# Three steps of shared experts among the first attention's rounds, and 26 instead of 18 sums of gathered rows left to the second attention

## Chip, cores and metric

One core of one Trainium2 chip runs the whole program, in float32, as one launch. The metric is the device time of one launch in microseconds; the time given for a kernel is the median of several runs.

## What is computed

Two decoder layers run on x of 4 x 1024 rows of 256 columns (NT = 4096 rows), with a context of 4 x 77 rows. A layer is an attention over the rows, a cross attention to the context and a mixture of experts, each with a residual and a layer norm behind it:

```python
x = _layernorm(x + _L0_attn_ref(x, ...))            # retention, 8 heads
x = _layernorm(x + _L0_xattn_ref(x, ctx, ctx, ...)) # 16 heads, 77 context rows
x = _layernorm(x + _L0_ffn_ref(x, ...))             # 64 experts, top 8, and 2 shared experts
x = _layernorm(x + _L1_attn_ref(x, ...))            # linear attention with a memory
x = _layernorm(x + _L1_xattn_ref(x, ctx, ctx, ...))
x = _layernorm(x + _L1_ffn_ref(x, ...))             # 8 gated experts, top 2

# in _L0_ffn_ref
h = jax.nn.silu(xf @ W1 + B1) @ W2 + B2             # one routed expert, 256 -> 64 -> 256
routed = sum over experts of cw[:, None] * h        # cw: weight of the expert, 0 unless in the row's top 8
shared = jnp.sum(jax.vmap(shared_mlp)(sw1, sb1, sw2, sb2), axis=0)   # 2 experts, 256 -> 512 -> 256, all rows
return routed + shared
```

## The kernel before

The rows are cut into 8 steps (STEPS) of 512 rows (128 of each of the 4 batches). The program has four phases, one behind the other, with some work let across the borders.

**First attention** (`attention_phase` with layer 0). The list SEQUENCE0 (L208) names the stages of a round, each with how many rounds ahead its step is; `steady` (L165) writes the rounds out, so that retention of step n, cross attention of step n-1, the router of step n-2 and the scatter of step n-3 share a round. All engines go through that one order. The stages that the change touches or stands beside: "cwt" and "b2" (expert weights turned, times the routed experts' second bias, plus the shared bias, into the tile `x2s`, which is the start value "base" of the feed phase's output and goes to memory by rows), "qk", "mx" (scores, L1186), "kt", "ret", "sc" (L1199 and L1202, scores of the cross attention), "mix" (L1069 and L1074), "pv" (L1212), L1057 (retention's part "ret"), and "put", in which GpSimd scatters each row eightfold into `lists`, the rows sorted by expert (L597, from round 3 on). SyncE's queue fills `lists` with zeros ahead of that (20 stores of 2 MB), loads the rows of later steps and stores x2, its transpose and the routes. A job's PSUM bank comes from one of two rings (`bank_jobs`: "wide" for "ret", "mx" and "sc", otherwise "narrow"). The prefetch of the routed experts' first weights (`prefetch(sp, 0)`, 4 MB) is issued at the phase's start. At its end `with_units` puts the first 8 units of the shared experts.

**A unit** (class `SharedExperts`) is one 128-column slice of the shared experts' 1024 hidden columns for one step: `inward` (L110, two matmuls of 512 columns, counted as four instructions in the profile), `activate` (L118, Silu on ScalarE) and `outward` (L127, four matmuls of 256 columns, counted as eight). Eight units (UNITS) make a step, 64 units (TOTAL) all; after the eighth, VectorE adds the result to base (L1697, "base"), and base goes back to memory ("send").

**Feed phase** (`feed_phase`, order by `feed_order` L1268). First 20 units (FIRST_UNITS), then 80 quads. A quad is four pages of 128 sorted rows: transposed on TensorE (L1716), times the first weights (L1728), Silu, times the second weights (L1739), stored to `results`. From quad 24 on (`begun`), a unit stands behind four of each five quads, a "weigh" (the second weights scaled, L1684 to L1690) behind each, and a sum behind six of seven. A sum adds one of the eight experts' results to a step's 512 rows: GpSimd gathers 4 x 128 rows of `results` (L1441, four DMA_INDIRECT for a sum, after a `rest` of L158), VectorE multiplies them by the weights and adds them (L1456, four instructions); after eight sums a step is done and its layer norm follows, so there are 64 sums. The first sum of step s waits until 24 + 8s quads are stored. LATE = STEPS*K0 - 18 = 46 sums are in this phase:

```python
units(FIRST_UNITS)
for j in range(QUADS0):
    order.append(("quad", j))
    ...
        weights(1)
        units(0 if (j - begun) % 5 == 0 else 1)
    if j >= begun + 2 and (j - begun) % 7:
        sums(1)
```

**Second attention** (`attention_phase` with layer 1, order SEQUENCE1). `with_late` puts the sums that the feed phase left, 18 here, behind named stages of its first rounds (the list `behind`); GpSimd's gathers for them run three sums ahead (AHEAD).

**Gated experts** (`gated_phase`): 8 experts of layer 1, matmuls of L2067 and L2079.

## Time and profile before

| | us |
|---|---|
| median of three runs | 1869.29 |
| lowest and highest | 1869.01, 1887.16 |
| span of the profiled execution | 1981.9 |
| profiled execution against the median | 112.6 longer |

The profiled execution is one launch with the hardware profiler on, and its span is the time from its first to its last instruction; the profile's times are of that launch. By the starts of its lines the first attention lies at 41 to about 600 us, the first units' end at 685, quads 0 to 23 at 685 to 776, quads 24 to 79 at 776 to 1107, the end of the feed phase to 1171, the second attention up to about 1500 and the gated experts behind it. PE is TensorE, DVE VectorE, ACT ScalarE, POOL GpSimd, SP SyncE. PEclk is the TensorE clock granted, 1.00 being 2.4 GHz and 0.5 being 1.2 GHz; "issue" as the releaser of a wait means that the engine waited for nothing that the profile shows.

### The profile page before, as it was taken

The page shows a single profiled execution, that of the slowest core. Times are in us where ns is not written, and L with a number is a line of the kernel's source. Part 1 is how long each engine was busy: PE and PEld are TensorE (multiplying, and loading weights), DVE is VectorE, ACT ScalarE, POOL GpSimd, SP SyncE. Part 2 cuts the span into 40 slices and gives each one's busy share as a digit, 9 for nine tenths or more (in the row PEclk, how much of TensorE's full clock was granted, in tenths as well). Part 3 has the DMA queues.
Part 4 walks back from the last instruction along what each step waited for, and adds up shares of the span by engine and source line. Part 5 has one row for each costly group of instructions (what it writes and reads, how often), then busy time and mean ns, then how long its engine had stood idle before and what let it go on. Part 6 is the DMA issues. An engine that isn't in the chain of part 4 may idle for free.

```text
span 1981.9 us, 45543 instructions
## 1 busy us (share of the span) xinstructions
PE 1687.5 (85%) x17739; PEld 1329.8 (67%) x17739; DVE 1165.2 (59%) x3228; ACT 623.2 (31%) x957; POOL 892.7 (45%) x1000
## 2 busy tenths in 40 slices
PE   6788888887689889998998478889977599999994
PEld 4566665666566567666676355667666499999994
DVE  4576655665432177776656456788765245655564
ACT  1232322222231277454555223445432111111110
POOL 0017556655758102888888856333323102222223
PEclk9999989998689999999998779999987699999997
DMA  9416543555448899888998922113111512333332
GB/s 325 150 46 199 184 150 116 190 169 191 146 147 237 219 304 295 285 278 273 297 294 290 317 78 82 57 65 121 69 39 65 164 49 76 91 94 98 98 94 69
DMA packets 269634, 322.61 MB, mean 163 GB/s; under 512 B 25083, under 2 KB 245487, under 8 KB 268655
## 3 DMA queue, kind: packets, MB, share of 16 engines
q1 hardware_dynamic: 234559, 226.38, 36.1%
q0 software_dynamic: 33024, 92.32, 14.4%
q8 instruction: 144, 2.36, 0.5%
q10 hardware_dynamic: 1840, 1.00, 0.2%
q14 instruction: 67, 0.55, 0.1%
HBM read 157.22 MB, written 162.40 MB: 161 GB/s over the span
## 4 chain that ended last, share of the span: by engine, by line
PE 68%; DVE 10%; issue 6%; DMA 6%; ACT 4%; POOL 3%; another core or an unknown queue 2%; SPq 1%; DVEq 1%; POOLq 0%; ACTq 0%
PE wide L2067 13%; PE d_yp L2079 6%; PE wide L110 4%; PE wide L127 4%; PE wide L1199 4%; PE wide L1202 3%; PE wide L1728 3%; PE e_yp L1739 3%; PE wide L1186 3%; PE bank L1033 3%; PE bank L1212 3%; PE bank L1219 2%; PE e_xp L1716 2%; PE bank L1105 2%
## 5 line engine op out<-in xcount | busy, mean ns | idle before, releaser
L1441 POOL DMA_INDIRECT big<-results,slots x256 | 263.4, 1029 | 202.1 <-DMA results<-e_y 125.5
L2067 PE MATMUL wide<-d_xt,d_ws 128*128 128x128 f32 x2272 | 279.0, 277 | 0.6 <-issue 0.6
L2067 PEld LDWEIGHTS wide<-d_xt,d_ws 128*128 128x128 f32 x2272 | 272.7, 193 | 4.5 <-issue 1.0
L597 POOL DMA_INDIRECT lists<-big,slots x160 | 159.6, 997 | 116.7 <-DVE slots L961 70.3
L663 ACT ACTIVATE pt<-wide 77x2048 f32<-77x2048 f32 x64 | 119.8, 1871 | 196.5 <-PE wide L1202 118.7
L1936 POOL DMA_INDIRECT d_picked<-results,slots x64 | 64.0, 1001 | 182.0 <-DMA results<-d_y 168.7
L1967 ACT ACTIVATE d_gate<-wide 128x512 f32<-128x512 f32 x71 | 42.4, 597 | 323.9 <-PE wide L2067 323.9
L2079 PE MATMUL d_yp<-d_wd,d_h 128*128 x568 | 134.2, 379 | 0.0
L1456 DVE SCALAR_TENSOR_TENSOR big<-big,weights 128x256 f32<-128x256 f32 x256 | 108.9, 487 | 41.6 <-DMA big<-results,slots 28.2
L110 PE MATMUL wide<-shared_sx,shared_sw 128*128 128x512 f32 x256 | 126.3, 616 | 7.7 <-DMA shared_sx<-res_t 5.2
L127 PEld LDWEIGHTS wide<-shared_sw,shared_sh 128*128 128x128 f32 x512 | 97.3, 191 | 45.1 <-issue 29.6
L127 PE MATMUL wide<-shared_sw,shared_sh 128*128 128x256 f32 x512 | 121.4, 380 | 3.6 <-DVE big L1697 3.6
L158 POOL TENSOR_TENSOR rest_ones<-rest_ones 128x4 f32<-128x4 f32 x108 | 121.0, 1120 | 2.0
L554 POOL TENSOR_TENSOR rs<-mv,eps 128x4 f32<-128x4 f32 x32 | 6.4, 199 | 234.9 <-DVE mv L712 234.1
L1212 PE MATMUL bank<-pt,vals 77*32 77x128 f32 x2048 | 89.6, 293 | 25.3 <-issue 15.4
L2079 PEld LDWEIGHTS d_yp<-d_wd,d_h 128*128 128x128 f32 x568 | 102.6, 190 | 11.0
L1998 DVE COPY d_ws<-big 128x1024 f32 x142 | 92.3, 693 | 27.5 <-issue 26.4
L2016 DVE TENSOR_TENSOR d_h<-d_gate,wide 128x512 f32<-128x512 f32 x71 | 48.7, 686 | 97.7 <-PE wide L2067 97.7
L1587 ACT ACTIVATE e_xt<-e_xp 128x1024 f32<-128x1024 f32 x80 | 81.9, 1024 | 76.5 <-PE e_xp L1716 48.7
L1716 PE MATMUL e_xp<-e_ident,e_x 128*128 128x128 f32 x640 | 86.9, 280 | 15.8 <-DMA e_x<-lists 12.2
L1199 PE MATMUL wide<-x1t,keys 32*77 32x128 f32 x1024 | 69.7, 315 | 35.8 <-issue 13.6
L1728 PE MATMUL wide<-e_xt,e_w1s 128*64 128x128 f32 x1280 | 89.4, 283 | 12.5 <-DVE e_w1s L1633 11.0
(280 smaller groups left out, 3488.8 us busy)
## 6 DMA issues: line engine op xcount, KB each, us to landing
lists<-zero SPq DMA_DIRECT2D x20, 2048.0 KB, 14.6
e_x<-lists SPq DMA_DIRECT2D x80, 512.0 KB
results<-e_y SPq DMA_DIRECT2D x80, 512.0 KB
d_x<-lists SPq DMA_DIRECT2D x71, 128.0 KB
results<-d_y SPq DMA_DIRECT2D x71, 128.0 KB
e_w<-in_L_w SPq DMA_DIRECT2D x2, 4096.0 KB
shared_sw<-in_x_t SPq DMA_DIRECT2D x32, 128.0 KB
x<-in_x SPq DMA_DIRECT2D x8, 512.0 KB
```

The source lines that it names most:

```text
L110: ins = nc.tensor.matmul(sp_h, self.sw1[:, c, u * P:(u + 1) * P], self.sx[:, s % 2, c], start=c == 0, stop=c == KC - 1)
L127: ins = nc.tensor.matmul(sp_y[b // 2][:, b % 2 * DM:(b % 2 + 1) * DM], self.sh[:, n % 2, b * P:(b + 1) * P], self.sw2[:, u], start=u == 0 ...
L158: step(self.nc.gpsimd.tensor_tensor(self.ones[:, 1], self.ones[:, 0], self.ones[:, 0], ALU.pow))
L597: pool.indirect_dma_start(out=lists, out_offset=bass.IndirectOffsetOnAxis(ap=slots[:, b, i, k:k + 1], axis=0), in_=z2[i % 3][:, b, :], in_ ...
L663: empties(nc.scalar.activation(pt[0:CTX, p % 2].rearrange("k (j n) -> k j n", j=4), ps[0:CTX], ACT.Exp, scale=score_scale), job)
L1199: mm(out[0:CTX, r, n * P:(n + 1) * P], keys[quarter(r), p, c, h * CTX:(h + 1) * CTX], qt[quarter(r), c, toks(p)], start=True, stop=False, ...
L1212: ins = mm(out[quarter(r), at:at + P], vals[:, p, c * 8 + 2 * r + h], pt[0:CTX, p % 2, of:of + P], start=True, stop=True)
L1441: pool.indirect_dma_start(out=picked[:, c % NG, b, :], out_offset=None, in_=results[0:-(-PAGES_OF_STEP[s] // 4) * 4 * R0, :], in_offset=ba ...
L1716: ins = tr(xp[:, h, (a * KC + c) * P:(a * KC + c + 1) * P], x[:, j % NX, h, a, c * P:(c + 1) * P], ident[:])
L1728: ins = mm(hp[h * H0:(h + 1) * H0, a * R0:(a + 1) * R0], w1s[:, j % NW1, h, a, c], xt[:, j % 2, h, a, c], start=c == 0, stop=c == KC - 1)
L2067: ins = mm(out[T % 2][:, a * P:(a + 1) * P], ws[:, T % NW, n, c, a * P:(a + 1) * P], xt[:, T % 2, c], start=c == 0, stop=c == KC - 1)
L2079: ins = mm(yp[T % 2][:, 0:DM], h[:, T % 2, c * P:(c + 1) * P], wd_flat[:, bass.ds(e * (HC * DM) + c * DM, DM)], start=c == 0, stop=c == HC ...
```

## The change

1. The shared experts of steps 0 to 2 (SOON = 3, 24 units) are computed in rounds 3 to 8 of the first attention, a group of four units in each (FOUR, GROUPS = 6). A group is four jobs "win" (inward of one unit, Silu on ScalarE into `gh`) and two jobs "wtwo" (outward of four units for two batches, eight matmuls of 256 columns, then VectorE adds it to `gbase`). They use banks of the narrow ring. Their weights (2 MB) are loaded once more into a half-buffer that the feed phase's first weights use later; for that, these weights' prefetch (4 MB) moves from the start of the phase to behind the last "wtwo". Base of a step is read back into `gbase`, and the sum goes to `mid`.
2. The units in the first attention's end and in the feed phase are those of steps 3 to 7, so 40 in all. Among the quads a unit stands behind one quad of four. Sums stand behind seven of ten quads.
3. LATE is STEPS*K0 - 26: 38 sums in the feed phase, 26 in the second attention. The list `behind` gets six places more in the first rounds.

```diff
-TOTAL = STEPS * UNITS
+SOON = 3
+FOUR = UNITS // 2
+GROUPS = SOON * UNITS // FOUR
+TOTAL = (STEPS - SOON) * UNITS
...
-    behind = [("x0t", 0, 1), ("sig", 0, 0)]
+    behind = [("x0t", 0, 1), ("sig", 0, 0), ("num", 0, 1), ("x0t", 1, 1), ("sig", 1, 0)]
     for i in range(4):
-        behind += [("x1t", i, 1), ("q", i, 1), ("mx", i, 1), ("mx", i, 3)]
+        behind += [("num", i + 1, 1), ("x1t", i, 1), ("q", i, 1), ("mx", i, 1), ("mx", i, 3)]
...
-    ("wout", 2, 0), ("wout", 2, 1), ("cwt", 3, 0), ("put", 3, 1), ("qk", 0, 0), ("x1t", 1, 0), ("x1t", 1, 1),
+    ("wout", 2, 0), ("wout", 2, 1), ("cwt", 3, 0), ("put", 3, 1), ("win", 3, 0), ("qk", 0, 0), ("x1t", 1, 0), ("x1t", 1, 1),
...
-            prefetch(sp, 0)
             if first:
                 sp.wait_ge(pool_ready, 3)
+            else:
+                prefetch(sp, 0)
...
+            def load_group(s):
+                for b in range(NB):
+                    at = b * SEQ + s * P
+                    sp.dma_start(gx[:, :, b * P:(b + 1) * P],
+                                 dst_t[:, at:at + P].rearrange("(c p) n -> p c n", p=P)).then_inc(gx_in, 16)
...
                 if n == 1:
                     sp.dma_start(units.sb1[:], d["sb1"]).then_inc(units.sb1_in, 16)
+                    sp.dma_start(gw2, d["sw2"].rearrange("e (c p) n -> p (e c) n", p=P)).then_inc(units.sw2_in, 16)
+                    for e in range(ES):
+                        sp.dma_start(gw1[:, :, e * HS:(e + 1) * HS], d["sw1"][e].rearrange("(c p) n -> p c n", p=P))\
+                            .then_inc(units.sw1_in, 16)
...
+                if n >= 2 and n % 2 == 0 and n // 2 - 1 < SOON:
+                    s = n // 2 - 1
+                    if s:
+                        filled(sp, ("win", 2 * s - 1, FOUR - 1))
+                    sp.wait_ge(sent_cols, 64 * (s + 1))
+                    load_group(s)
+                if n >= 3 and n % 2 == 1 and (n - 3) // 2 < SOON:
+                    load_gbase((n - 3) // 2)
...
+                if n >= 4 and n % 2 == 0 and n // 2 - 2 < SOON:
+                    send_gbase(n // 2 - 2)
+                    if n // 2 - 2 == SOON - 1:
+                        filled(sp, ("wtwo", GROUPS - 1, 1))
+                        prefetch(sp, 0)
...
+                if stage == "win":
+                    ...
+                    ps = filled(act, job)
+                    empties(nc.scalar.activation(gh[:, at], ps[:], ACT.Silu, bias=units.sb1[:, u:u + 1]), job)
...
+                if stage == "wtwo":
+                    pair = slice(2 * p, 2 * p + 2)
+                    dve.wait_ge(gbase_in, 16 * (i // 2 + 1))
+                    ps = filled(dve, job)
+                    ...
+                    ins = nc.vector.tensor_tensor(gbase[:, pair], ps[:].rearrange("p (b n) -> p b n", b=2),
+                                                  gbase[:, pair], ALU.add)
+                    empties(ins, job)
...
+                if stage == "win":
+                    u = i % 2 * FOUR + p
+                    ...
+                    for c in range(KC):
+                        ins = mm(out[:], gw1[:, c, u * P:(u + 1) * P], gx[:, c], start=c == 0, stop=c == KC - 1)
+                    fills(ins, job)
+                if stage == "wtwo":
+                    for n in range(FOUR):
+                        emptied(pe, ("win", i, n))
+                    for bb in range(2):
+                        for n in range(FOUR):
+                            u = i % 2 * FOUR + n
+                            ins = mm(out[:, bb * DM:(bb + 1) * DM], gh[:, u, toks(2 * p + bb)], gw2[:, u],
+                                     start=n == 0, stop=n == FOUR - 1)
+                    fills(ins, job)
...
-LATE = STEPS * K0 - 18
+LATE = STEPS * K0 - 26
...
-            units(0 if (j - begun) % 5 == 0 else 1)
-        if j >= begun + 2 and (j - begun) % 7:
+            units(0 if (j - begun) % 4 else 1)
+        if j >= begun + 2 and (j - begun) % 10 < 7:
             sums(1)
...
-                sp.dma_start(base, by_step[s * P:(s + 1) * P]).then_inc(base_in, 16)
+                sp.dma_start(base, by_step[(SOON + s) * P:(SOON + s + 1) * P]).then_inc(base_in, 16)
```

The order on TensorE shows the move. The first place is the first attention in a round with scatters, behind "cwt"'s transposes (first row); `shared_sw,wqk` are "qk", `keys,x1t` "mx". Before:

```order
L1241 MATMUL bank_0<-ident,cw 64x128 x4
L1033 MATMUL bank_0<-shared_sw,wqk 128x512 x2
L1105 MATMUL bank_0<-ident,x 128x128 x8
L1186 MATMUL wide<-keys,x1t 128x154 x8
L1033 MATMUL bank_0<-shared_sw,wqk 128x512 x2
L1246 MATMUL bank_0<-b_0,cwt 128x256 x4
L1186 MATMUL wide<-keys,x1t 128x154 x8
L1033 MATMUL bank_0<-shared_sw,wqk 128x512 x2
```

and now:

```order
L1327 MATMUL bank_0<-ident,cw 64x128 x4
L1313 MATMUL bank_0<-big 128x512 x2
L1100 MATMUL bank_0<-shared_sw,wqk 128x512 x2
L1172 MATMUL bank_0<-ident,x 128x128 x8
L1253 MATMUL wide<-keys,x1t 128x154 x8
L1100 MATMUL bank_0<-shared_sw,wqk 128x512 x2
L1313 MATMUL bank_0<-big 128x512 x2
L1332 MATMUL bank_0<-b_0,cwt 128x256 x4
```

The rows of L1313 are two "win", one before the first "qk", one behind the second.

The second place is in the same rounds, from the last "sc" ahead of "mix" (L1069 and L1074 before, L1136 and L1141 now) and, after the dots, from the end of "mix" to the next "sc". Before:

```order
L1202 MATMUL wide<-shared_sh,sel 77x128 x4
L1069 MATMUL bank_0<-shared_sw,state 32x128 x4
L1074 MATMUL bank_0<-big,shared_sx 32x128 x4
```

```order
L1074 MATMUL bank_0<-big,shared_sx 32x128 x4
L1057 MATMUL wide<-shared_sw 128x128 x16
L1212 MATMUL bank_0<-pt,vals 32x128 x16
L1199 MATMUL wide<-x1t,keys 77x128 x4
L1202 MATMUL wide<-shared_sh,sel 77x128 x4
```

and now:

```order
L1269 MATMUL wide<-shared_sh,sel 77x128 x4
L1321 MATMUL bank_0<-big 128x256 x8
L1136 MATMUL bank_0<-shared_sw,state 32x128 x4
L1141 MATMUL bank_0<-big,shared_sx 32x128 x4
```

```order
L1141 MATMUL bank_0<-big,shared_sx 32x128 x4
L1124 MATMUL wide<-shared_sw 128x128 x16
L1279 MATMUL bank_0<-pt,vals 32x128 x16
L1321 MATMUL bank_0<-big 128x256 x8
L1266 MATMUL wide<-x1t,keys 77x128 x4
L1269 MATMUL wide<-shared_sh,sel 77x128 x4
```

Each of the two rows of L1321 is a "wtwo" of eight matmuls; nothing else has moved.

The third place is the feed phase among its later quads; L1716, L1728 and L1739 (now L1804, L1816 and L1827) are a quad, L110 and L127 (now L113 and L130) a unit. Before:

```order
L1716 MATMUL e_xp<-e_ident,e_x 128x128 x8
L1728 MATMUL wide<-e_xt,e_w1s 64x128 x8
L1739 MATMUL e_yp<-e_w2s,e_ht 128x256 x4
L110 MATMUL wide<-shared_sx,shared_sw 128x512 x2
L127 MATMUL wide<-shared_sw,shared_sh 128x256 x4
L1716 MATMUL e_xp<-e_ident,e_x 128x128 x8
L1728 MATMUL wide<-e_xt,e_w1s 64x128 x8
L1739 MATMUL e_yp<-e_w2s,e_ht 128x256 x4
L110 MATMUL wide<-shared_sx,shared_sw 128x512 x2
L127 MATMUL wide<-shared_sw,shared_sh 128x256 x4
```

and now:

```order
L1804 MATMUL e_xp<-e_ident,e_x 128x128 x8
L1816 MATMUL wide<-e_xt,e_w1s 64x128 x8
L1827 MATMUL e_yp<-e_w2s,e_ht 128x256 x4
L113 MATMUL wide<-shared_sx,shared_sw 128x512 x2
L130 MATMUL wide<-shared_sw,shared_sh 128x256 x4
L1804 MATMUL e_xp<-e_ident,e_x 128x128 x8
L1816 MATMUL wide<-e_xt,e_w1s 64x128 x8
L1827 MATMUL e_yp<-e_w2s,e_ht 128x256 x4
L1804 MATMUL e_xp<-e_ident,e_x 128x128 x8
L1816 MATMUL wide<-e_xt,e_w1s 64x128 x8
L1827 MATMUL e_yp<-e_w2s,e_ht 128x256 x4
L1804 MATMUL e_xp<-e_ident,e_x 128x128 x8
```

A unit stood behind four of five quads, and now stands behind one of four.

## Rows read from the trace of the kernel before

**Rows 1.** Page: span and busy share of TensorE
```profile
span 1981.9 us, 45543 instructions
...
PE 1687.5 (85%) x17739; PEld 1329.8 (67%) x17739; DVE 1165.2 (59%) x3228; ACT 623.2 (31%) x957; POOL 892.7 (45%) x1000
```

**Rows 2.** Windows by stage of the program, all engines
```profile
core 0: us, PE busy (x) PEld busy (x) DVE busy (x) ACT busy (x) POOL busy (x), PEclk, DMA share, GB/s
95.00:148.20 53.20, 47.63 (x819) 37.84 (x819) 38.83 (x97) 18.17 (x24) 5.10 (x10) 0.97 0.14 40
...
350.50:417.80 67.30, 56.76 (x835) 42.96 (x831) 41.55 (x104) 18.67 (x25) 40.39 (x46) 0.92 0.48 156
...
485.00:558.00 73.00, 52.70 (x533) 39.76 (x534) 33.84 (x98) 15.40 (x19) 47.10 (x52) 0.68 0.61 203
...
745.00:765.00 20.00, 18.14 (x180) 13.53 (x176) 14.84 (x49) 15.09 (x25) 0.00 (x0) 1.00 1.01 323
...
776.00:1107.00 331.00, 304.27 (x2176) 217.87 (x2174) 214.76 (x710) 166.68 (x255) 268.58 (x257) 0.97 0.89 285
1107.00:1171.00 64.00, 31.41 (x195) 23.68 (x195) 33.81 (x102) 11.65 (x23) 40.21 (x46) 0.69 0.59 199
...
1386.50:1427.00 40.50, 38.27 (x588) 28.93 (x588) 32.00 (x103) 18.22 (x28) 12.88 (x18) 0.96 0.20 74
1600.00:1900.00 300.00, 300.00 (x2286) 288.78 (x2285) 169.89 (x329) 47.38 (x108) 70.25 (x92) 1.00 0.29 86
```

**Rows 3.** The same view, the second attention's rounds with sums
```profile
1171.00:1346.00 175.00, 152.00 (x2285) 112.02 (x2286) 132.31 (x392) 69.79 (x105) 86.38 (x100) 0.93 0.24 74
```

**Rows 4.** Waits of TensorE, 282.8 to 485, three rounds
```profile
PE wide L1199 <- issue: 6.4, 8, 1.9
PE bank L1069 <- issue: 4.2, 11, 1.0
```

**Rows 5.** Timeline of TensorE in the round 350.5 to 417.8
```profile
364.53 0.81 PE L1186 MATMUL wide<-keys,x1t 32*128 32x154 f32 x16 [0.34 <-issue]
...
377.74 1.17 PE L1057 MATMUL wide<-shared_sw 32*128 32x128 f32 x32 [0.89 <-issue]
...
389.35 0.27 PE L1074 MATMUL bank<-big,shared_sx 128*32 128x128 f32 x1 [0.30 <-issue]
...
393.02 2.11 PE L1057 MATMUL wide<-shared_sw 32*128 32x128 f32 x30 [0.65 <-issue]
...
398.66 0.72 PE L1199 MATMUL wide<-x1t,keys 32*77 32x128 f32 x8 [1.67 <-issue]
```

**Rows 6.** Timeline of TensorE in round 2, like places
```profile
124.03 0.40 PE L1199 MATMUL wide<-x1t,keys 32*77 32x128 f32 x8
...
126.12 0.40 PE L1074 MATMUL bank<-big,shared_sx 128*32 128x128 f32 x8
```

**Rows 7.** Timeline of TensorE among the quads
```profile
870.67 1.98 PE L110 MATMUL wide<-shared_sx,shared_sw 128*128 128x512 f32 x4
872.49 1.89 PE L127 MATMUL wide<-shared_sw,shared_sh 128*128 128x256 f32 x8
874.21 1.04 PE L1716 MATMUL e_xp<-e_ident,e_x 128*128 128x128 f32 x8
...
877.27 1.98 PE L110 MATMUL wide<-shared_sx,shared_sw 128*128 128x512 f32 x4
```

**Rows 8.** Gathers (L1441) and outward (L1739), 776 to 1107
```profile
L1441 POOL DMA_INDIRECT big<-results,slots x189: 942/966/1887, 780.6 to 1106.9; - x189
...
L1739 PE MATMUL e_yp<-e_w2s,e_ht x448: 373/376/792, 775.7 to 1104.6; 64*128 64x256 f32 x150
```

**Rows 9.** Adds of the sums (L1456), 1171 to 1346
```profile
L1456 DVE SCALAR_TENSOR_TENSOR big<-big,weights x48: 443/477/2455, 1169.2 to 1301.2; 128x256 f32<-128x256 f32 x48
```

**Rows 10.** DMA of the stretch 776 to 1107
```profile
DMA packets 76820, 94.49 MB, mean 285 GB/s; under 512 B 5297, under 2 KB 69496, under 8 KB 76782
```

**Rows 11.** Timeline of ScalarE at the first unit
```profile
583.16 1.28 ACT L118 ACT_TABLE_LOAD   x1
```

More of the change, by code:

```diff
@@ L169, in steady @@
         for stage, ahead, part in sequence:
-            if 0 <= n - ahead < STEPS:
+            if 0 <= n - ahead < (GROUPS if stage in ("win", "wtwo") else STEPS):
                 order.append((stage, n - ahead, part))
@@ L209 @@
     ("wo", 1, 0), ("wo", 1, 1), ("put", 3, 0), ("v", 0, 0), ("v", 0, 1), ("ln1", 1, 0),
[L210 removed]
[4 rows of a table removed]
+    ("wout", 2, 0), ("wout", 2, 1), ("cwt", 3, 0), ("put", 3, 1), ("win", 3, 0), ("qk", 0, 0), ("x1t", 1, 0), ("x1t", 1, 1),
+    ("mx", 1, 0), ("ln2", 2, 0), ("qk", 0, 1), ("win", 3, 1), ("b2", 3, 0), ("b2", 3, 1), ("mx", 1, 1), ("res", 1, 0), ("put", 3, 2),
+    ("qk", 0, 2), ("x2t", 2, 0), ("x2t", 2, 1), ("mx", 1, 2), ("win", 3, 2), ("put", 3, 3), ("qk", 0, 3), ("mx", 1, 3), ("put", 3, 4),
+    ("win", 3, 3), ("kt", 0, 0), ("ret", 0, 0), ("kt", 0, 1), ("put", 3, 5), ("mt", 1, 0), ("rt", 2, 0), ("put", 3, 6), ("put", 3, 7),
+    ("sc", 1, 0), ("wtwo", 3, 0), ("mix", 0, 0), ("top", 2, 0), ("ret", 0, 1), ("pv", 1, 0), ("wtwo", 3, 1), ("sc", 1, 1),
+    ("mix", 0, 1), ("up", 0, 0),
     ("rank", 2, 0), ("sc", 1, 2), ("pv", 1, 1), ("sc", 1, 3), ("pv", 1, 2), ("pv", 1, 3),
@@ L229, in attention_phase @@
                     spare=None, route=None, block=None,
-                    over=(), kept=(), late_on_pool=None, late_on_vector=None, units=None):
+                    over=(), kept=(), late_on_pool=None, late_on_vector=None, units=None, soon_memory=None, mid=None):
     first = layer == 0
@@ L336, in attention_phase @@
             qt = x1t
+            gw1 = soon_memory[:, 0:2048].rearrange("p (c n) -> p c n", c=KC)
+            gw2 = soon_memory[:, 2048:4096].rearrange("p (u n) -> p u n", u=UNITS)
+            gh = soon_memory[:, 4096:8192].rearrange("p (k n) -> p k n", k=2 * FOUR)
+            gx = spare[:, 5120:6144].rearrange("p (c n) -> p c n", c=KC)
+            gbase = spare[:, 4096:5120].rearrange("p (b n) -> p b n", b=NB)
         else:
@@ L479, in _, with load_gbase, send_gbase @@
             load_t(1)
-            prefetch(sp, 0)
             if first:
                 sp.wait_ge(pool_ready, 3)
+            else:
+                prefetch(sp, 0)
             out_rows = dst.rearrange("(b s) n -> s b n", b=NB)
+            def load_group(s):
[3 more added lines that the diff above has]
+                                 dst_t[:, at:at + P].rearrange("(c p) n -> p c n", p=P)).then_inc(gx_in, 16)
+            def load_gbase(s):
+                sp.wait_ge(sent_rows[0], 16 * (s + 1))
+                if s:
+                    sp.wait_ge(gbase_sent, 16 * s)
+                else:
+                    sp.wait_ge(ready, READY)
+                sp.dma_start(gbase, out_rows[s * P:(s + 1) * P]).then_inc(gbase_in, 16)
+            def send_gbase(s):
+                for p in range(2):
+                    emptied(sp, ("wtwo", 2 * s + 1, p))
+                sp.dma_start(mid.rearrange("(b s) n -> s b n", b=NB)[s * P:(s + 1) * P], gbase)\
+                    .then_inc(gbase_sent, 16)
             for n in range(STEPS + 3 if first else 0):
@@ L629, in _ @@
                     units.activate(nc, act, i, wide[:, 0])
+                if stage == "win":
+                    u, at = i % 2 * FOUR + p, i % 2 * FOUR + p
+                    if i == 0 and p == 0:
+                        act.wait_ge(units.sb1_in, 16)
+                    if i >= 2 and p == 0:
+                        filled(act, ("wtwo", i - 2, 1))
+                    ps = filled(act, job)
+                    empties(nc.scalar.activation(gh[:, at], ps[:], ACT.Silu, bias=units.sb1[:, u:u + 1]), job)
                 if stage in ("v", "kt"):
@@ L1237, in _ @@
                     fills(ins, job)
+                if stage == "win":
+                    u = i % 2 * FOUR + p
+                    if i == 0 and p == 0:
+                        pe.wait_ge(units.sw1_in, 16 * ES)
+                        pe.wait_ge(units.sw2_in, 16)
+                    if i % 2 == 0 and p == 0:
+                        pe.wait_ge(gx_in, 64 * (i // 2 + 1))
+                    for c in range(KC):
[10 more added lines that the diff above has]
+                    fills(ins, job)
                 if stage == "cwt":
@@ L1253, in attention_phase @@
             over += [(blank[k], 16 * len(blanks(k))) for k in range(STEPS)]
+            over += [(gbase_sent, 16 * SOON)]
             return over, put_of[:2], (slot_done, STEPS)
@@ L1547, in _ @@
                     load_route((n + 1) // 6)
-                if kind == "unit" and n and n % UNITS == 0 and shared < STEPS:
+                if kind == "unit" and n and n % UNITS == 0 and SOON + shared < STEPS:
                     sp.wait_ge(experts.full, n)
@@ L1769, in feed_phase @@
         kept = [(stored[s % NA], 16 * (s // NA + 1)) for s in range(STEPS)]
-        over = [(sent[n], 16 * len(range(n, QUADS, NY))) for n in range(NY)] + [(base_sent, 16 * STEPS)]
+        over = [(sent[n], 16 * len(range(n, QUADS, NY))) for n in range(NY)] + [(base_sent, 16 * (STEPS - SOON))]
         return over, kept, late_on_pool, late_on_vector
@@ L2145, in decoder @@
                 nc, sems, shared, 0, layer0, a["x"], a["x_t"], res1, res1_t, E0, load_layer0, lists0, slots0, weights0, page_ends0,
-                halves[1], route0, block, units=experts)
+                halves[1], route0, block, units=experts, soon_memory=halves[0], mid=mid)
             last_x2 = halves[1][:, 6144:7168].rearrange("p (b n) -> p b n", b=NB)
```

22 lines of the change are left out of this document (14 added, 8 removed), and 4 rows, old and new, of the table SEQUENCE0.

## The prediction

> **What bounds the kernel now.** I read the page first, then windows by stage, then TensorE's waits and timeline in single rounds, then the gathers and the DMA traffic. TensorE is busy for 85% of the span [rows 1], but what limits it differs from stage to stage, and the change moves work from one stage to two others.
>
> In a round of the first attention with scatters, 350.5 to 417.8 us, TensorE is busy for 56.76 of 67.3 us, at a mean granted clock of 0.92; VectorE, ScalarE and GpSimd are busy for 42, 19 and 40 us [rows 2]. So 10.5 us of a round are TensorE's idle time, and none of it is one long wait: the largest entries of three rounds together are "issue", 6.4 and 4.2 us in small pieces [rows 4]. In round 2, which has no scatters, TensorE idles 53.2 - 47.63 = 5.6 us at clock 0.97 [rows 2], and the same L1074 stands without a gap [rows 6] that has one of 0.30 us in the round with scatters [rows 5]. Round 8, 485 to 558, idles 20.3 of 73 us at 0.68 [rows 2].
>
> Among the quads, 776 to 1107, two engines are near full: TensorE is busy for 304 of 331 us, and GpSimd gathers from 780.6 to 1106.9 [rows 2, 8]. The 189 gathers are 47 sums, so one sum takes (1106.9 - 780.6) / 47 = 6.94 us of GpSimd's time. 94.49 MB go through DMA at 285 GB/s [rows 10]; the most that a stretch with the queues full shows is 323 GB/s, 745 to 765, share 1.01 [rows 2]. In the second attention a round without sums takes 40.5 us, and the four rounds from 1171 to 1346 take 175 us [rows 2, 3].
>
> **What the change moves.** A unit costs TensorE 874.21 - 870.67 = 3.54 us (two inward, four outward matmuls) and a quad 877.27 - 874.21 = 3.06 us [rows 7]. Twenty-four units leave the feed phase: 24 x 3.54 = 85 us of TensorE's time. They come back as six groups of four, 14.2 us each, with the same matmul shapes.
>
> *Rounds 3 to 7.* What a group costs is 14.2 us less the idle time that it fills. Three of the named waits lie where a job is put: 0.34 us at L1186, 0.89 at L1057 and 1.67 at L1199 [rows 5], together 2.9. The sixteen matmuls of a "wtwo" are long ones (256 columns) ahead of short ones that pause at "issue", and the four pauses of 0.3 and one of 0.65 from 389 to 393 [rows 5] may close, as may those behind the second "wtwo": I take 3.1. So a round grows by 14.2 - 2.9 - 3.1 = 8.2 us, five of them by 41. The bounds: all of the 10.5 idle is filled, and the clock is full: a mean of 0.92 over 67.3 us is 10.8 us at half, which cost 5.4, so 14.2 - 10.5 - 5.4 = -1.7 a round. Nothing is filled: 14.2. I take a value nearer the upper end because most idle pieces stand away from the new jobs. The other engines' share is hidden: four Silu and two adds a round are some 4 us for engines with 48 and 25 us free [rows 2]. ScalarE changes its table twice more a round, at 1.28 us each [rows 11], beside those 48.
>
> *Round 8.* It idles 20.3 us [rows 2], waiting on transfers and on the other engines. I let it fill 10 of 14.2: +4, bounds -2 and +14.
>
> *The new transfers.* The groups load 2 MB of weights early, and per step 0.5 MB of rows and 0.5 MB of base in and out, in rounds whose DMA share is about 0.5 [rows 2]; a load is issued a round before it is used. The SyncE queue gets waits for "win" and "wtwo" jobs: behind them stand the next rows' loads and the route stores, which have most of a round. The 4 MB prefetch starts around 540 us and is needed at 685: at 150 GB/s, roughly what the rounds show, it takes 27 us. I put these at nothing; 0 to 10 us if a load is late once.
>
> *Quads 24 to 79.* There are 56 of them (448 outward instructions [rows 8], eight for each). TensorE's work becomes 56 x 3.06 + 13 x 3.54 = 217 us, so TensorE no longer sets this stretch. GpSimd then does: eight sums fewer, 331 - 8 x 6.94 = 275 us. The traffic falls by eight sums of 0.52 MB, by three steps' base in, base out and rows (1.57 MB each), and by one load and store of the sums' own base (1.05), to about 84.5 MB: 262 us at 323 GB/s, 296 at 285. GpSimd's 275 lies between; its implied 307 GB/s has been reached in the row at 745. I take 275 and book -56, bounds -35 (traffic at today's rate) and -69 (traffic at the highest, if sums run faster too). The tail from 1107 to 1171 I leave as it is, TensorE idling 33 of 64 us there [rows 2].
>
> The Trainium skill, "DMA: Bandwidth & Descriptors", section "Specifications", gives about 358 GB/s as a core's share of HBM. No stretch here was that fast; by that figure the traffic would be an estimated 236 us and no limit, while by the trace's 323 it is 262.
>
> *Second attention.* It takes eight sums more. The 48 adds from 1171 to 1301 [rows 9] are 12 sums, and those four rounds take 175 - 4 x 40.5 = 13 us more than rounds without sums: 1.1 us a sum, so +9. Bounds: 0, since GpSimd and VectorE have idle time there (86 and 132 of 175 us busy [rows 3]), and 8 x 4 x 0.48 = 15, all the adds in the open.
>
> **The sum.** 41 + 4 - 56 + 9 = -2 us on the profiled execution's 1981.9. The median is 112.6 us shorter than that span, and no view tells in which phase; I carry the difference over unchanged: 1869.3 - 2, about 1867. In other words, TensorE's work is the same; the change gains what it fills of the first attention's idle time and pays what it leaves idle in the feed phase.
>
> **Rivals.**
>
> *The clock also recovers (faster).* The rounds' L1199 takes 0.72 us for eight at 398.66 [rows 5] and 0.40 in round 2 [rows 6]: that part of the round runs at 1.2 GHz, after the pauses at 389 to 398. With a "wtwo" of dense long matmuls in front of and behind them the granted clock may stay at 2.4. That is 5.4 us a round, 27 in five: 1867 - 27 = 1840. Against it: the rounds' pauses also stand where no job is put, and round 2 shows 0.97, not 1. The Trainium skill, "TensorE: Matmul & The Clock Gate", Part 1, says that "the default state is throttled, and activity releases the throttle"; by that, dense matmuls there would help, and the trace agrees so far that the low clock stands behind the pauses.
>
> *The idle time of the rounds is the profiled execution's own (slower).* The gated experts keep TensorE busy for 300 of 300 us and the quads for 304 of 331 [rows 2], so little of the 112.6 us by which the profiled launch is longer than the median can lie there; it must lie largely where TensorE idles, in the attention phases. If a timed launch has no idle time in rounds 3 to 8, a group costs its full 14.2 us, six of them 85 instead of 45: 1867 + 40 = 1907. From a mean of 11 us a round on it is over 1% slower. For it speaks that sum; against it, that round 2 is profiled too and has few gaps, so that the pauses come with the scatters, which every launch has.
>
> *Traffic binds the quads (about the same).* Already at a share of 0.89 [rows 2], the quads run no faster than 285 GB/s: 296 us, 21 more than taken: 1888.
>
> *The groups are late or harm the scatters.* A wait on `gbase` or the late 4 MB stops TensorE once: some 20 to 40 us, 1890 to 1905.
>
> **How the numbers follow.** My forecast has a chance of 0.42, the clock's recovery 0.22, the full cost of the groups 0.20, the traffic 0.11, a late load 0.05. A measurement of this kernel tells about 1%, 18.7 us, from no change. Of the forecast's 0.42 its own bounds of some 20 us either way put 0.10 below 1850.6 and 0.05 above 1888, and 0.27 within; the clock's recovery puts 0.22 on the faster side, less 0.01 for a recovery in part; the full cost gives 0.18 to the slower, 0.02 to the same; of the traffic's 0.11, 0.06 are within and 0.05 slower; the late load splits 0.03 and 0.02. That makes 0.31 faster, 0.38 same and 0.31 slower (0.10 + 0.21; 0.27 + 0.01 + 0.02 + 0.06 + 0.02; 0.05 + 0.18 + 0.05 + 0.03). The likeliest case alone would be 1845 to 1890; to leave out no more than 2 in 10 the range reaches past 1840 and to the full cost's 1907: 1834 to 1908.
>
> **What would show it.** In the changed profile rounds 3 to 7 should take about 75 us instead of 67, with TensorE busy for about 71; at 1.2 GHz in the same stretch the clock has not recovered, and a mean of 0.97 or more says that it has. The gathers should still stand back to back, at about 6.9 us a sum, and the last of 38 sums' gathers should start about 56 us sooner after the first quad with sums; gathers that wait between quads say that traffic or the quads bind. TensorE should idle over 50 us there. The rounds of the second attention with sums should be 43 to 46 us, one or two more of them. I am wrong if rounds 3 to 7 grow by under 3 or over 12 us, or if the stretch of the 56 quads stays over 300.

## The result and the profile after

The changed kernel takes 1904.1 us, median of four runs, the kernel before 1871.6 beside it: a ratio of 1.0168 (95% interval 1.0131 to 1.0204), slower by 1.7%. 1867 was predicted, with a range from 1834 to 1908 and 0.31 for slower by over 1%. The time lies inside the range, near its slow end; but the forecast was no change, and a loss was measured.

The page of the changed kernel: span, busy times and granted clock in 40 slices:

```profile
span 1905.5 us, 45608 instructions
...
PE 1625.1 (85%) x17739; PEld 1299.1 (68%) x17739; DVE 1168.2 (61%) x3234; ACT 639.6 (34%) x969; POOL 894.9 (47%) x1000
...
PEclk9999999999999999899997778899996899999997
```

Its span, 1905.5, agrees with its timed runs. The one of the kernel before did not: 1981.9 [rows 1] against 1870. So the kernel before was profiled once more (first experiment); that launch, span 1869.0, is the one to compare with:

```profile
span 1869.0 us, 45543 instructions
...
PE 1612.6 (86%) x17739; PEld 1293.2 (69%) x17739; DVE 1168.9 (63%) x3228; ACT 626.6 (34%) x957; POOL 894.9 (48%) x1000
...
PEclk9999999997999999999997699999995999999997
```

Its clock has no dip in rounds 0 to 7 of the first attention; the 7 in the tenth slice, 420 to 467 us, is in round 8. The windows of this second profile by stage (us, then busy time and instructions of TensorE, its weight loads, VectorE, ScalarE and GpSimd, granted clock, DMA share, GB/s): a round of the first attention with scatters, round 8 with the first units, quads 24 to 79, and the second attention's rounds 1 to 4. A round of the second attention is counted from the first matmul of L1114 (L1181 in the changed kernel) of one step to that of the next.

```profile
249.00:303.50 54.50, 48.70 (x845) 38.55 (x841) 41.92 (x103) 18.95 (x26) 40.03 (x46) 1.00 0.61 199
412.30:602.00 189.70, 162.06 (x1238) 115.68 (x1231) 74.94 (x230) 47.63 (x63) 127.92 (x137) 0.91 0.76 224
...
692.10:1022.70 330.60, 306.23 (x2179) 219.75 (x2176) 215.76 (x710) 169.17 (x255) 269.23 (x253) 0.96 0.88 283
...
1071.20:1096.30 25.10, 17.61 (x128) 11.38 (x128) 16.24 (x43) 7.89 (x16) 11.32 (x14) 0.86 0.21 64
1096.30:1132.20 35.90, 31.23 (x560) 22.98 (x556) 30.93 (x75) 15.67 (x21) 27.77 (x30) 1.00 0.34 101
1132.20:1173.20 41.00, 36.45 (x590) 27.69 (x586) 35.11 (x108) 18.54 (x28) 24.82 (x30) 0.99 0.28 80
1173.20:1219.10 45.90, 37.82 (x598) 29.05 (x594) 39.66 (x129) 18.38 (x28) 19.57 (x24) 0.95 0.22 72
```

And the same stages of the changed kernel, which answer to [rows 2, 3]:

```profile
266.40:331.20 64.80, 62.40 (x889) 47.33 (x882) 42.93 (x105) 23.97 (x32) 40.75 (x45) 1.00 0.56 184
460.80:651.60 190.80, 170.24 (x1287) 117.75 (x1279) 75.72 (x232) 52.75 (x69) 120.96 (x130) 0.96 0.80 243
...
748.40:1026.60 278.20, 224.62 (x1878) 166.72 (x1876) 193.85 (x652) 150.32 (x230) 223.87 (x211) 0.92 0.90 297
...
1074.80:1116.60 41.80, 21.02 (x126) 13.99 (x126) 22.21 (x67) 7.89 (x16) 32.22 (x34) 0.63 0.34 101
1116.60:1161.50 44.90, 35.90 (x558) 26.59 (x554) 30.20 (x75) 15.67 (x21) 35.72 (x37) 0.85 0.31 92
1161.50:1206.90 45.40, 40.52 (x592) 30.42 (x588) 38.58 (x114) 18.72 (x28) 35.13 (x40) 0.89 0.34 98
1206.90:1254.00 47.10, 38.02 (x598) 29.49 (x594) 42.35 (x138) 18.39 (x28) 23.06 (x28) 0.96 0.25 79
```

At the same places of both programs (the end of "mix" in rounds 2 and 7, the start of the first quad's transposes and of the second attention's first L1114 or L1181) the spans divide into

| stage | before, second profile | after | difference | predicted |
|---|---|---|---|---|
| up to round 2 | 139.0 | 136.9 | -2.1 | 0 |
| rounds 3 to 7 | 273.3 | 323.9 | +50.6 | +41 |
| round 8 and the first units | 189.7 | 190.8 | +1.1 | +4 |
| quads to the second attention | 457.5 | 411.5 | -46.0 | -56 |
| from there to the end | 809.5 | 842.4 | +32.9 | +9 |
| sum | 1869.0 | 1905.5 | +36.5 | -2 |

Every forecast term has the right sign. Rounds 3 to 7, the quads and the second attention are each some 10 us or more worse than forecast, and the largest miss, 24 us of 38, is the second attention's.

### The profile page after: what moved, and what is told of

Read it like the earlier page. It is cut to its first block, busy times and chain, and to the rows that moved or that the text cites. A ratio compares the mean times of both kernels' runs of the same rounds, so it can differ in the third digit from the quotient of the medians.

```text
span 1905.5 us, 45608 instructions
## 1 busy us (share of the span) xinstructions
PE 1625.1 (85%) x17739; PEld 1299.1 (68%) x17739; DVE 1168.2 (61%) x3234; ACT 639.6 (34%) x969; POOL 894.9 (47%) x1000
## 4 chain that ended last, share of the span: by engine, by line
PE 61%; POOL 13%; DVE 8%; DMA 6%; issue 6%; ACT 4%; SPq 2%; DVEq 0%; POOLq 0%; ACTq 0%
PE wide L2155 13%; POOL big L1529 8%; PE d_yp L2167 6%; PE bank L1100 3%; PE wide L1266 3%; PE bank L1286 3%; POOL rest_ones L161 2%; PE bank L1321 2%; PE wide L1269 2%; PE bank L1313 2%; PE wide L1253 2%; PE wide L113 2%; PE wide L130 2%; PE bank L1279 2%; PE bank L1106 2%
## 5 line engine op out<-in xcount | busy, mean ns | idle before, releaser
L1816 PE MATMUL wide<-e_xt,e_w1s 128*64 128x128 f32 x1280 | 95.0, 295 | 39.4 <-DVE e_w1s L1721 39.2
L1816 PEld LDWEIGHTS wide<-e_xt,e_w1s 128*64 128x64 f32 x1280 | 74.3, 145 | 54.6 <-DVE e_w1s L1721 43.9
L1804 PE MATMUL e_xp<-e_ident,e_x 128*128 128x128 f32 x640 | 89.2, 284 | 21.8 <-DMA e_x<-lists 20.1
L1804 PEld LDWEIGHTS e_xp<-e_ident,e_x 128*128 128x128 f32 x640 | 71.8, 144 | 47.2 <-DMA e_x<-lists 30.6
L1827 PE MATMUL e_yp<-e_w2s,e_ht 64*128 64x256 f32 x640 | 97.4, 425 | 1.5 <-ACT e_y L1675 1.5
L1675 ACT ACTIVATE e_y<-e_yp 128x1024 f32<-128x1024 f32 x80 | 81.9, 1024 | 47.7 <-PE e_yp L1827 47.7
L658 POOL DMA_INDIRECT lists<-shared_sw,slots x64 | 62.4, 974 | 68.8 <-PE wide L1269 28.1
L1726 DVE COPY e_w2s<-e_w 64x257 f32 x320 | 83.5, 300 | 6.5 <-PE e_yp L1827 3.4
## 6 DMA issues: line engine op xcount, KB each, us to landing
lists<-zero SPq DMA_DIRECT2D x20, 2048.0 KB, 14.6
```

The costliest lines, as they stand in the source:

```text
L1675: return nc.scalar.activation(out, in_, ACT.Copy)
L1804: ins = tr(xp[:, h, (a * KC + c) * P:(a * KC + c + 1) * P], x[:, j % NX, h, a, c * P:(c + 1) * P], ident[:])
L1816: ins = mm(hp[h * H0:(h + 1) * H0, a * R0:(a + 1) * R0], w1s[:, j % NW1, h, a, c], xt[:, j % 2, h, a, c], start=c == 0, stop=c == KC - 1)
L1827: ins = mm(yp[:, h, a * DM:(a + 1) * DM], ht[lanes, j % 2, a], w2s[lanes, j % NW2, a, 0:DM], start=True, stop=True)
```

## Experiments

**A second profile of the kernel before** (no edit).

> The kernel before, unchanged, for a second profile: the one shown had a span of 1981.9 us where timed launches take 1870, while the changed kernel's profile (1905.5) agrees with its times. Theory A (the idle time of the first attention's rounds belonged to that one profiled launch, so a group costs all of its 14 us): span near 1870, rounds 3 to 7 near 51 us, with TensorE idle for under 5 us in each. Theory B (the rounds do idle and the groups fill it, and the loss lies in the feed phase or the second attention): rounds 3 to 7 near 60 us, TensorE idle for some 8 us in each.

Measured: 1870.9 us, a span of 1869.0. Round 3 takes 55.7 us and rounds 4 to 7 take 54.4 each, with TensorE busy for 48.6 at full clock, so 5.8 us idle: between the two theories' figures, nearer to theory A's. TensorE's waits in three of these rounds (line, waited for, us in total, times, longest), first before, then after:

```profile
PE wide L1199 <- DVE big L788: 7.1, 3, 2.4
PE bank L1212 <- ACT pt L663: 3.2, 3, 1.1
PE wide L1199 <- ACT pt L663: 2.9, 3, 1.0
PE wide L1057 <- DVE shared_sh L854: 2.4, 3, 0.8
```

```profile
PE bank L1279 <- ACT pt L721: 3.2, 3, 1.1
PE wide L1266 <- ACT pt L721: 2.9, 3, 1.0
```

These waits name no "issue" pause any more: those of [rows 4, 5], and the low clock behind them, belonged to the launch profiled first. In the changed kernel the waits on VectorE (7.1 and 2.4 us in three rounds) are gone, those on ScalarE stand. TensorE is busy for 62.4 us of 64.8, that is 13.8 more; 3.4 us of idle time were filled, and a round grows by 10.4.

**The sums alone**, in the kernel before:

```diff
-LATE = STEPS * K0 - 18
+LATE = STEPS * K0 - 26
```
with the longer list `behind` of the change (25 places instead of 18, so seven more and not six).

> The kernel before with only the sums moved: 38 sums in the feed phase, 26 in the second attention. Theory A': the feed phase is bound by GpSimd's gathers and TensorE about equally, so without eight sums it ends when TensorE does, some 25 to 35 us sooner, and the second attention pays 9 of it: 1845 to 1855. Theory B': the end of the feed phase is bound by the quads with their units, and nothing but the second attention's part is seen: 1875 to 1885.

Measured: 1888.4 us, ratio 1.0092 (1.0067 to 1.0116). The stretch from the first quad to the second attention falls by 14.7 us (457.5 to 442.8), half of what the first theory expects, and what follows grows by 24.1 (809.5 to 833.6). That is above both expectations. TensorE, with all its units, does not let the feed phase end sooner: from quad 24 to the last quad it is busy for 303.4 of 320.4 us.

**The groups left out**, in the changed kernel (their weights and rows not loaded either):

```diff
-            if 0 <= n - ahead < (GROUPS if stage in ("win", "wtwo") else STEPS):
+            if 0 <= n - ahead < (0 if stage in ("win", "wtwo") else STEPS):
...
-                    emptied(sp, ("wtwo", 2 * s + 1, p))
+                sp.wait_ge(gbase_in, 16 * (s + 1))
```

> The changed kernel without the groups: the shared experts of steps 0 to 2 are left out of the computation, their base still goes through the same loads and stores. Theory A: 6 x 14 = 84 us less than the changed kernel, about 1820. Theory B (the groups fill idle time): 45 us less or fewer, about 1860.

Measured: 1855.6 us, 48.5 below the changed kernel. The six groups cost 8.1 us each in the mean, close to theory B and to the 45 us that the prediction's sum had for them, not 84. In the profiles 42.7 us of it lie before the first quad, and 6.7 in the second attention and behind (835.7 us), which this edit does not touch. Even without the work of 24 units the kernel is only 0.9% faster than before (ratio 0.9914, 0.9885 to 0.9944).

**18 sums late in the changed kernel:**

```diff
-LATE = STEPS * K0 - 26
+LATE = STEPS * K0 - 18
```
with the old list `behind`.

> The changed kernel with 18 sums left to the second attention, as before. If GpSimd's gathers bind the feed phase there: 8 x 6.94 = 56 us more in it and 9 less in the second attention, about 1950. If the quads or the traffic bind it: about 1895 to 1915.

Measured: 1926.3 us, 22 above the changed kernel: the feed phase is 51.0 us longer (462.5 against 411.5), the rest 33.7 shorter (808.7 against 842.4). So GpSimd's gathers do bind the feed phase once the units are gone, at 51.0 / 8 = 6.4 us a sum, and it is the second attention's price that was missed, 33.7 instead of 9. This price varies between launches: with the same 26 sums, the stretch from the second attention to the end is 833.6 us in the profile of the sums alone, 835.7 without the groups and 842.4 in the changed kernel, so eight sums cost 24 to 34 us there. With the three runs before, the four corners are: neither part 1870, units alone 1926, sums alone 1888, both 1904. As built here, either part alone loses, since TensorE and GpSimd bind the feed phase almost equally: the sums alone shorten it by 14.7 us, the units alone not at all, both by 46. One reservation: in this run the sums still follow seven of ten quads, so the quads take as long as in the changed kernel (376.8 and 375.4 us), and 52 gathers instead of 21 stand behind the last one. A rhythm made for 46 sums was not tried without the units.

**The late sums spread out**, two instead of five in rounds 0 and 1, and one round more at the end:

```diff
-    behind = [("x0t", 0, 1), ("sig", 0, 0), ("num", 0, 1), ("x0t", 1, 1), ("sig", 1, 0)]
-    for i in range(4):
-        behind += [("num", i + 1, 1), ("x1t", i, 1), ("q", i, 1), ("mx", i, 1), ("mx", i, 3)]
+    behind = [("x0t", 0, 1), ("sig", 0, 0)]
+    for i in range(5):
+        behind += [("x1t", i, 1), ("q", i, 1), ("mx", i, 1), ("mx", i, 3)] + ([("mx", i, 0)] if i < 2 else [])
```

> The changed kernel with its 26 late sums spread over one more round: two instead of five behind stages of the second attention's rounds 0 and 1, five in rounds 2 and 3, four in rounds 4 to 6. Theory C (in the first rounds, GpSimd's queue of gathers delays the layer norm's scale that TensorE waits for, so where the sums stand matters): the second attention gives back 10 to 18 of the 33 us that eight sums cost it, so 1886 to 1894. Theory D (a sum costs 4 us there wherever it stands): 1904, no change.

Measured: 1912.5 us, ratio 1.0211 (1.0175 to 1.0247; the changed kernel's 1.0131 to 1.0204 overlaps); from the second attention's first round to the end 841.4, as before the edit (842.4). Round 1 falls from 41.8 to 27.0 us, but round 5, which had no sums, rises from 37.6 to 52.0:

```profile
1239.70:1291.70 52.00, 40.88 (x596) 31.45 (x592) 39.36 (x125) 18.61 (x28) 34.37 (x39) 0.87 0.29 90
```

Theory C falls in its part on the place: the price moves along with the sums.

**One step instead of three, in rounds 7 and 8**, 22 sums late, with `behind` nearly as in the run before and the other sums behind seven of nine quads:

```diff
-SOON = 3
+SOON = 1
...
-    ("win", 3, 0) ... ("wtwo", 3, 1)
+    ("win", 7, 0) ... ("wtwo", 7, 1)
...
-            units(0 if (j - begun) % 4 else 1)
+            units((j - begun + 1) % 2)
...
-LATE = STEPS * K0 - 26
+LATE = STEPS * K0 - 22
```

> The changed kernel with one step of shared experts moved instead of three (SOON = 1), its two groups in rounds 7 and 8, a unit behind every second quad, and 22 sums late, spread as in e5_spread. Theory A'' (a group in a full round costs 10 us, one in round 8 next to nothing; the feed phase gains about as much for 8 units and 4 sums as GpSimd is relieved, 25 us; the sums cost 1 to 4 us each): 11 - 25 + 4 to 16, 1860 to 1873. Theory B'' (the first rounds are not special, groups cost 8 us on average wherever they stand, and a sum 4): 1870 + 16 - 25 + 16, about 1877.

Measured: 1878.6 us, ratio 1.0034 (1.0013 to 1.0056). The round with the first group and the stretch of round 8 with the second, by windows:

```profile
356.40:421.50 65.10, 62.67 (x891) 47.51 (x887) 43.07 (x105) 24.04 (x32) 48.25 (x52) 1.00 0.55 179
421.50:612.40 190.90, 170.05 (x1287) 117.54 (x1276) 75.70 (x232) 52.69 (x69) 120.81 (x130) 0.96 0.81 243
```

The former takes 65.1 us instead of 54.4, the latter 190.9 against 189.7: as theory A'' has it, a group in a full round costs over 10 us and the one in round 8 next to nothing. The feed phase gains 21.5 (436.0), the end loses 14.6 (824.1), 3.7 us for each of four sums. The total itself is next to the 1877 of theory B''; beside it the kernel before took 1873.9, so it does not tell the two theories apart, and the two rounds do.

**The same in rounds 8 and 9** ("win", 8 and "wtwo", 8; the base's store and the prefetch follow in SyncE's iteration 9, one later than in the run before).

> As e7_one_step_r7, but the two groups in rounds 8 and 9, where the first attention runs out. Theory A'': both groups fill idle time, 1852 to 1866, some 8 us below e7. Theory B'': as e7, about 1877; or more, if the groups delay the last scatters.

Measured: 1899.3 us, ratio 1.0143 (1.0116 to 1.0170). The first quad starts 26.8 us later than before. TensorE's longest wait from 407 us on, and VectorE's longest on a transfer in this time, stand at the phase's border:

```profile
PE wide L130 <- DVE big L1784: 20.2, 1, 20.2
```

```profile
DVE e_slots_f L1730 <- DMA res<-x2s: 19.7, 1, 19.7
```

Neither theory's time came; of the two, only theory B'' had named a delay. The last store of x2s is late. It stands behind the base's store and the 4 MB prefetch on SyncE's queue, which wait for the group in round 9; that this is the reason was not tried apart.

**21 sums late in the kernel before**, three more places at the list's end (`range(5)` for `range(4)`).

> The kernel before with 21 instead of 18 sums left to the second attention, the three more behind stages of its rounds 6 and 7 (no groups). If GpSimd and TensorE bind the feed phase within 15 us of each other, as e1_sums_alone says (15 us sooner for eight sums), three sums already give the 15 us, and at 1 to 4 us a sum the whole comes to 1858 to 1867. If a sum in the second attention always costs what it saves: 1870.

Measured: 1874.7 us, ratio 0.9998 (0.9978 to 1.0019), no change and not the 1858 to 1867 of the first theory: the feed phase gains 6.6 us and the end loses 11.5 in its profile.

**10 sums late in the kernel before.**

> The kernel before with 10 instead of 18 sums left to the second attention (54 in the feed phase). From the start of the second attention's first transposes to the end it is 810 us with 18 late sums, 821 with 21, 824 with 22, 842 with 26. If a sum costs the same everywhere (3.5 to 4 us): 778 to 782. If only sums beyond what its rounds can hide cost: 800 to 810. The whole is longer by 8 x 6.94 less that.

Measured: 1907.2 us, ratio 1.0191 (1.0131 to 1.0250); from the second attention's first round to the end 793.3, between the two expectations. So 8 sums from 10 to 18 cost 16.2 us, 2.0 each, and 8 from 18 to 26 cost 33, 4.1 each. Its round 4, which has no sums left, takes 36.3 us, where the kernel before has 45.8.

**Which engine's work is the price: eight sums' adds, gathers, or both.** In the changed kernel, for the sums 41 to 48:

```diff
-            for b in range(NB):
+            for b in range(1 if 41 <= n < 49 else NB):
                 ins = nc.vector.scalar_tensor_tensor(...
...
-            for b in range(NB):
+            for b in range(1 if 41 <= c < 49 else NB):
                 pool.indirect_dma_start(...
```

> The changed kernel, with three of four adds (VectorE) of eight sums in the second attention's first rounds left out of the computation; their gathers stay. If VectorE's time is the price of a sum: 8 x 3 x 0.48 = 12 us or more less, down to 33 less: 1871 to 1892. If GpSimd's: 1900 to 1904.

> The changed kernel, with three of four gathers (GpSimd) of the same eight sums left out of the computation; the adds stay. If GpSimd's queue is the price of a sum: 20 to 33 us less, 1871 to 1884. If VectorE's: 1896 to 1904.

> The changed kernel, with three of four gathers and three of four adds of the same eight sums left out. What is left of eight sums is a quarter of each, so by either theory some 25 to 33 us less than the changed kernel, 1871 to 1880; more than that would say that something else of the move costs nothing or less.

Measured: 1902.2 without the adds, 1894.1 without the gathers, 1898.0 without both, against 1904.1. From the second attention to the end, the profiles have 840.3, 831.7 and 831.3 us against 842.4. Adds: next to nothing. Gathers: 10 us, not the 20 to 33 expected; and leaving out both gives no more than the gathers alone (what these two runs differ by lies before the second attention's first round), not the 25 to 33 expected. The rounds say why: GpSimd gathers three sums ahead, so the eight stand before and in round 1, which falls from 41.8 to 35.0 us (30.5 without both), while rounds 2 to 4 keep their full gathers and their 42 to 47 us.

**Gathers, or adds, of the three lengthened rounds.** The same edits with 44 <= c < 59 for the gathers, and with 41 <= n < 56 for the adds.

> The changed kernel, with three of four gathers (GpSimd) of 15 sums left out of the computation: those that GpSimd issues in the second attention's rounds 1 to 3; all adds stay. If GpSimd's queue sets these rounds (41.8, 44.9 and 45.4 us in the changed kernel): near 30, 36 and 38 us, together some 25 us less, about 1880. If not: 10 us less as with the first eight sums, about 1894.

> The changed kernel, with three of four adds (VectorE) of the 15 sums left out that stand in the second attention's rounds 0 to 3; all gathers stay. If GpSimd's queue sets these rounds: at most 5 us less, 1899 to 1904. If VectorE does: 15 x 3 x 0.48 = 22 us less, about 1882.

Measured: 1879.1 us without the gathers, 25 less; 1900.7 without the adds, 3 less. Rounds 1 to 3 without the gathers, by windows:

```profile
1075.40:1106.70 31.30, 21.73 (x126) 14.30 (x126) 24.18 (x67) 7.89 (x16) 21.21 (x22) 0.67 0.26 74
1106.70:1140.10 33.40, 30.93 (x562) 23.00 (x554) 30.00 (x75) 15.68 (x21) 12.97 (x15) 1.00 0.16 49
1140.10:1182.30 42.20, 37.38 (x594) 28.74 (x586) 36.85 (x115) 18.50 (x28) 26.25 (x31) 0.96 0.28 81
```

and without the adds:

```profile
1079.70:1118.60 38.90, 17.72 (x128) 11.35 (x128) 15.28 (x49) 7.88 (x16) 30.34 (x33) 0.74 0.36 108
1118.60:1164.50 45.90, 36.30 (x559) 26.22 (x555) 24.49 (x60) 15.67 (x21) 36.43 (x39) 0.85 0.33 97
1164.50:1204.50 40.00, 37.12 (x591) 28.76 (x587) 36.20 (x108) 18.72 (x28) 30.80 (x36) 0.96 0.34 100
```

Without gathers GpSimd's busy time in round 2 falls from 35.7 to 13.0 us and the round from 44.9 to 33.4, at full clock; round 3 falls only to 42.2. Without adds VectorE's falls from 30.2 to 24.5 and the round stays at 45.9. So GpSimd's queue sets round 2 and most of the lengthening of round 1. From the second attention's start to the end 842.4 falls to 816.4 without the gathers, by 26 us, and to 831.9 without the adds, by 10.5, though that kernel's timed launches are only 3 us shorter. The 26 us are no share of the 33: rounds 1 to 3 have 24 gathers left here, where the kernel before has 37 and the changed kernel 66.

## Why the prediction was wrong

**The step that failed: "1.1 us a sum, so +9".** It measured 33.7 us for eight sums, 4.2 each, and 24 us in the least of the profiled launches. The prediction took 175 us from 1171 to 1346 for four rounds with sums and subtracted four rounds without sums of 40.5 us [rows 2, 3]. Two things are wrong in this.

First, 40.5 us is not what these rounds take without sums. With 10 late sums, rounds 3 and 4 have none and take 35.8 and 36.3 us. Nor are the first rounds of this phase full, since the later stages' steps are not in them yet: round 2 has 560 matmul instructions where round 4 has 598. Compared with 40.5 us, the sums looked almost free; those from 10 to 18 cost 2.0 us each.

Second, the next eight cost more than those before them, because of where they land. The window from 1171 on holds no more than the last 10 us of round 1, which ends at 1181 in the first profile. Yet GpSimd's gathers rise from 5 to 22 in round 1 (second profile and changed kernel), from 18 to 22 in round 2 and from 14 to 22 in round 3. Rounds 1 and 2 lasted 25.1 and 35.9 us and now last 41.8 and 44.9: 25.7 of the 32.9 us. The rounds with sums did come out near the 43 to 46 us that the prediction had named as a sign; what it had not seen is how short the first two were.

The bound of 15 us failed for a reason of its own: it priced the adds on VectorE alone. GpSimd's gathers were not in it, because GpSimd was busy for only 86 of 175 us [rows 3]. That share is a mean over rounds. In round 2 of the kernel before GpSimd already has no room: it is busy for 27.8 of 35.9 us, and nearly all the rest are its pauses beside gathers and one wait for ScalarE (the rows are GpSimd's waits from 1096.3 to 1132.2, second profile):

```profile
POOL big L1441 <- issue: 4.6, 15, 0.3
POOL x1b L585 <- ACT x L674: 2.2, 1, 2.2
POOL big L1441 <- POOL rest_ones L158: 1.4, 5, 0.3
```

In round 2 of the changed kernel GpSimd runs five sums of 6.1 to 6.3 us each, some 31 us, beside its own norms and stores, all in one order, for the 44.9 us of the round. What this does to TensorE in round 1 is a chain over four engines; the rows are the changed kernel's timeline (start, duration, engine, line). VectorE has the layer norm's means and variances:

```profile
1088.87 0.15 DVE L770 BATCH_NORM_AGGREGATE mv<-stats 128x2 f32<-128x6 f32 x1
```

GpSimd still has gathers ahead of the norm's scale (`rs`, L604 to L607), and reaches it 12 us later:

```profile
1100.18 0.95 POOL L1529 DMA_INDIRECT big<-results,slots  x1 [0.30 <-issue]
1101.16 0.21 POOL L604 TENSOR_TENSOR rs<-mv,eps 128x4 f32<-128x4 f32 x1
...
1102.73 0.19 POOL L607 TENSOR_TENSOR rs<-rs 128x4 f32<-128x4 f32 x1
```

In the second profile of the kernel before, GpSimd is there first and waits 9.9 us for VectorE:

```profile
1081.17 0.19 POOL L554 TENSOR_TENSOR rs<-mv,eps 128x4 f32<-128x4 f32 x1 [9.94 <-DVE mv L712]
```

In the changed kernel ScalarE then scales x, and TensorE goes on:

```profile
1102.96 2.08 ACT L732 ACTIVATE x<-x,rs 128x256 f32<-128x256 f32 x4 [18.76 <-POOL rs L607]
```

```profile
1104.19 2.07 PE L1172 MATMUL bank<-ident,x 128*128 128x128 f32 x8 [15.43 <-ACT x L732]
```

TensorE waited 15.4 us. Its clock had gone to the lower level at 1080.4, in a wait of 3.0 us before, and stayed there up to 1111.1 (0.50 in that stretch): the eight matmuls of L1172 take 2.07 us at 1104.19 and 1.04 at 1112.55. Round 1 has a mean clock of 0.63 and round 2 of 0.85, where the kernel before has 0.86 and 1.00; in round 2 nearly the same matmuls (558 and 560 instructions) keep TensorE busy for 35.9 instead of 31.2 us.

**Rounds 3 to 7: "14.2 less 2.9 less 3.1".** The group's price (13.8 measured, 14.2 forecast) and the filled waits (3.4 measured, 2.9 forecast, but on VectorE and not where the first profile had them) were about right. The 3.1 for closing pauses failed: the pauses were not there. The rival on the profiled launch said so: half of its premise holds, TensorE idles 5.8 us in a round, not 10.5 and not none. But its price does not: the groups cost 48.5 us, not 85. That it named 1907 and 1904 was measured is not its merit; the 33 us of the second attention stand in for what the groups did not cost.

**Round 8: "+4".** It measured +1.1. TensorE's idle time in this stretch fell by 7.1 us (27.6 to 20.6), and its busy time grew by 8.2 and not by 13.8, at a clock of 0.96 instead of 0.91; that the clock makes up the rest was not tried apart.

**The quads: "-56".** -46. GpSimd's gathers set the stretch, as forecast, with 46 sums before (second profile) and 38 after; the rows group the gathers of this stretch by line (durations in ns, then first and last start):

```profile
L1441 POOL DMA_INDIRECT big<-results,slots x184: 942/967/2218, 696.1 to 1016.7; - x184
```

```profile
L1529 POOL DMA_INDIRECT big<-results,slots x152: 942/965/2223, 749.3 to 1017.5; - x152
```

From first to last gather that is 320.6 and 268.2 us, -52.4, or 6.97 and 7.06 us a sum. The first gather is 3.6 us later after the first quad, and 2.8 are added behind the last one. TensorE now waits there for VectorE (38.1 us, where the second profile has 17.4), which does the weights' scaling and the adds in one order and itself waits for gathers (27.9 us, 42.1 in the second profile); that TensorE's waits come by this way is read from the lines alone. The rows are the changed kernel's waits from 748 to 1026, first TensorE's, then VectorE's:

```profile
PE wide L1816 <- DVE e_w1s L1721: 38.1, 14, 8.5
```

```profile
DVE big L1544 <- DMA big<-results,slots: 27.9, 13, 4.1
```

**The rivals.** The recovering clock has nothing to recover from: 1.00 in rounds 3 to 7 on both sides. Traffic does not bind the quads: 297 GB/s after, 283 before. TensorE's clock has a mean of 0.63 in round 1 of the second attention, where it waits longest. That a low clock stands behind its waits there is what the Trainium skill, "TensorE: Matmul & The Clock Gate", Part 1, says of the throttled default; the trace agrees. The new loads stopped nothing in the groups' rounds, where neither TensorE's nor VectorE's waits name a transfer.

**What stays open.** Round 3 stays at 42.2 us without its gathers, but with them it takes 42.2 in the run of the sums alone, so the 45.4 in the changed kernel's profile may belong to that launch. What the adds cost is open: 10.5 us by the profile without 15 sums' adds, 3 by the timed launches. That a different order on GpSimd, with the norm's scale ahead of the gathers, would win the time back was not tried. Nor was a version found that is faster than the kernel before: the best one that computes everything, with 21 late sums and no groups, is no different from it.

## To carry over

To price work added to a pipeline's rounds, compare a round with the same round without that work, not with another one: rounds in which the pipeline fills are shorter, and what stands in them looks free. An engine that serves several others in one order is not free because its mean share is half; ask in each round what short instruction, that others wait for, will stand behind the new work. And before idle time is counted as room, see that the profiled launch takes as long as the timed ones; where it is 6% longer, take the idle time as unknown.
